# Down products of two experts as three 16-bit products instead of one in float32

## The reference

```
h    = layernorm(attention @ Wo)
gate = softmax(h @ gate_w + gate_b)                      # 8 experts
hid  = gelu(einsum('bsd,edf->bsef', h, w1) + b1)         # up product, f = 512
out  = einsum('bsef,efd->bsed', hid, w2) + b2            # down product
moe  = einsum('bse,bsed->bsd', gate, out)
```

## Time and profile before

| | |
|---|---|
| Median of 3 runs | 1122.25 us (1120.18 to 1125.5) |
| Profiled execution, its own time | 1120.17 us |
| Its span, first to last instruction | 1118.4 us |
| Granted TensorE clock over the span | 0.986 |
| Busy: PE, PEld, DVE | 96%, 82%, 86% |
| Busy: ACT, POOL | 70%, 25% |

### The profile page before, as it was taken

One profiled execution on the slowest core, in us unless ns is written; L12 is line 12 of the kernel. 1 busy time (PEld: TensorE's weight loads), 2 busy tenths in 40 slices (PEclk: granted clock), 3 DMA queues, 4 the chain that ended last, 5 costly groups with the idle time before them and its releaser, 6 DMA issues.

```text
span 1118.4 us, 27576 instructions
## 1 busy us (share of the span) xinstructions
PE 1075.0 (96%) x10435; PEld 912.2 (82%) x10435; DVE 959.6 (86%) x2543; ACT 778.9 (70%) x1772; POOL 277.7 (25%) x328
## 2 busy tenths in 40 slices
PE   4877999999999999999999999999999999999997
PEld 1664888888888888888888888888888888888897
DVE  8988798898988989898898989889898888988763
ACT  5873948668595876859677594867759587685653
POOL 2340314224031231404123140412403132140200
PEclk9995999999999999999999999999999999999999
DMA  7010000000000000000000000000000000000000
GB/s 210 7 39 10 2 11 7 1 16 1 11 7 11 6 2 16 1 11 6 6 11 2 11 7 11 6 1 16 2 11 6 11 7 6 6 6 1 7 2 10
DMA packets 18722, 14.60 MB, mean 13 GB/s; under 512 B 2408, under 2 KB 16160, under 8 KB 18592
## 3 DMA queue, kind: packets, MB, share of 16 engines
q1 hardware_dynamic: 17680, 12.76, 3.8%
q10 hardware_dynamic: 912, 0.09, 0.1%
HBM read 10.75 MB, written 2.10 MB: 11 GB/s over the span
## 4 chain that ended last, share of the span: by engine, by line
PE 89%; DVE 4%; issue 3%; ACT 2%; POOL 1%; SPq 0%; DMA 0%; POOLq 0%; DVEq 0%; ACTq 0%
PE O L565 19%; PE O L468 14%; PE S L484 5%; PE U L547 5%; PE U L548 5%; PE U L549 5%; PE J L382 5%; PE S L449 4%; PE J L343 4%; PE U L449 4%; PE S L404 4%; PE J L344 3%; PE J L345 3%; PE S L400 3%; PE O L475 2%
## 5 line engine op out<-in xcount | busy, mean ns | idle before, releaser
L777 ACT ACTIVATE hid<-U,b1c 128x256 f32<-128x256 f32 x512 | 200.5, 474 | 174.8 <-PE U L549 174.7
L565 PE MATMUL O<-w2s,hid 128*128 128x128 f32 x2048 | 251.1, 276 | 0.0
L565 PEld LDWEIGHTS O<-w2s,hid 128*128 128x128 f32 x2048 | 238.6, 192 | 2.9
L928 POOL TENSOR_SCALAR_AFFINE_SELECT P<-P 128x512 f32<-128x512 f32 x128 | 85.0, 664 | 618.6 <-ACT P L750 618.5
L468 PEld LDWEIGHTS O<-Vx,P 128*128 128x128 f32 x1536 | 188.0, 192 | 30.2 <-issue 14.3
L468 PE MATMUL O<-Vx,P 128*128 128x66 f32 x1536 | 188.6, 273 | 3.6 <-POOL P L928 2.0
L1198 DVE TENSOR_TENSOR_SCAN st<-aexp,u 128x256 f32<-128x256 f32 x256 | 178.8, 698 | 0.4 <-issue 0.3
L920 POOL TENSOR_TENSOR raw<-raw,nr 128x512 f32<-128x512 f32 x124 | 132.8, 1097 | 134.9 <-DVE nr L1066 134.9
L1208 DVE SCALAR_TENSOR_TENSOR y<-st,bc,y 128x256 f32<-128x256 f32 x240 | 133.5, 556 | 8.5
L547 PE MATMUL U<-h2h,w1h 128*128 128x256 f16 x480 | 130.9, 273 | 0.0
L549 PE MATMUL U<-h2h,w1l 128*128 128x256 f16 x480 | 130.9, 273 | 0.0
(11 more groups left out here) (204 smaller groups left out, 2048.0 us busy)
## 6 DMA issues: line engine op xcount, KB each, us to landing
xin<-in_L_attn_x SPq DMA_DIRECT2D x16, 128.0 KB, 2.1
xres<-in_L_attn_x SPq DMA_DIRECT2D x16, 128.0 KB, 2.3
hid<-in_L_ffn_w SPq DMA_DIRECT2D x2, 1024.0 KB, 6.5
out_dram<-fin SPq DMA_DIRECT2D x16, 128.0 KB, 1.8
raw<-in_L_ffn_Wq SPq DMA_DIRECT2D x1, 512.0 KB, 4.7
raw<-in_L_ffn_Wk SPq DMA_DIRECT2D x1, 512.0 KB, 6.4
raw<-in_L_ffn_Wv SPq DMA_DIRECT2D x1, 512.0 KB, 7.4
wos<-in_L_ffn_Wo SPq DMA_DIRECT2D x1, 512.0 KB, 11.4
```

What stands on the lines that cost most here:

```text
L565: last = mm(O[e % 2][:, t * P:(t + 1) * P], hid[:, e % 2, m, t * P:(t + 1) * P], w2s[:, e * FC + m, :], start=(m == 0), stop=(m == FC - 1))
L777: fn(hid[:, e % 2, f % FC, :], U[q % 2][:, m * SEQ:(m + 1) * SEQ], ACT.Gelu_apprx_tanh, bias=b1c[:, f:f + 1], scale=1.0 / WS).then_inc(gel ...
```

## The change

For experts 0 and 1 (`NH = 2`) the down product is made from 16-bit halves, as the up product is. ACT copies the gelus' values of one expert, 128x1024, to 16 bits (`hidh`), DVE subtracts that from `hid` into `hidl`, and PE makes three 16-bit matmuls where one float32 matmul was. There is one buffer each of `hidh` and `hidl`, so the copy for expert 1 waits for expert 0's down block. The halves of `w2` are made once, and scaled by 64, which the gate's copy `gate64` takes out. Line numbers of the changed kernel differ.

```diff
+        hidh = sb("hidh", [P, FC, SEQ], F16)
+        hidl = sb("hidl", [P, FC, SEQ], F16)
+        w2h = sb("w2h", [P, NH * FC, D], F16)
+        w2l = sb("w2l", [P, NH * FC, D], F16)
+        gate64 = sb("gate64", [P, T, NH])
...
             def expert_down(s, e, weighed):
-                pe.wait_ge(gelu_done, s * NE * FC + FC * (e + 1))
+                if e < NH:
+                    pe.wait_ge(hid_low, s * NH + e + 1)
+                    pe.wait_ge(w2_low, 1)
+                else:
+                    pe.wait_ge(gelu_done, s * NE * FC + FC * (e + 1))
...
                 for t in range(T):
                     for m in range(FC):
-                        last = mm(O[e % 2][:, t * P:(t + 1) * P], hid[:, e % 2, m, t * P:(t + 1) * P],
-                                  w2s[:, e * FC + m, :], start=(m == 0), stop=(m == FC - 1))
+                        dst, f, q = O[e % 2][:, t * P:(t + 1) * P], e * FC + m, slice(t * P, (t + 1) * P)
+                        if e < NH:
+                            mm(dst, hidh[:, m, q], w2h[:, f, :], start=(m == 0), stop=False)
+                            mm(dst, hidh[:, m, q], w2l[:, f, :], start=False, stop=False)
+                            last = mm(dst, hidl[:, m, q], w2h[:, f, :], start=False, stop=(m == FC - 1))
+                        else:
+                            last = mm(dst, hid[:, e % 2, m, q], w2s[:, f, :], start=(m == 0), stop=(m == FC - 1))
...
+            def hidden_high(s, e):
+                act.wait_ge(gelu_done, s * NE * FC + FC * (e + 1))
+                from_one(act, w2_ready, s * NE + e if e > 0 else (s - 1) * NE + NH)
+                fn(hidh[:, :, :], hid[:, e % 2, :, :], ACT.Copy).then_inc(hid_high, 1)
...
+                    if not old and m == 5:
+                        act.wait_ge(d_w2, 16)
+                        fn(w2h[:, :, :], w2s[:, 0:NH * FC, :], ACT.Copy, scale=WS).then_inc(w2_high, 1)
...
+                    for t in range(T):
+                        V.tensor_scalar(gate64[:, t, :], ge[:, t, 0:NH], grs[:, t:t + 1], 1.0 / WS, ALU.mult,
+                                        ALU.mult).then_inc(o_vec, 1)
...
+            def hidden_low(s, e):
+                dve.wait_ge(hid_high, s * NH + e + 1)
+                V.tensor_tensor(hidl[:, :, :], hid[:, e % 2, :, :], hidh[:, :, :], ALU.subtract).then_inc(hid_low, 1)
+
+            def split_w2():
+                dve.wait_ge(w2_high, 1)
+                V.scalar_tensor_tensor(w2l[:, :, :], w2s[:, 0:NH * FC, :], WS, w2h[:, :, :], ALU.mult, ALU.subtract
+                                       ).then_inc(w2_low, 1)
...
+                    if i == 1 and k == 7:
+                        split_w2()
```

More of the change, by code:

```diff
@@ L24 @@
 NL = NP
+NH = 2
 VW = DH + 2
@@ L35 @@
 KN = 8
-KO, KOA = 17, 2
+KO, KOA = 19, 2
 KE = 9
@@ L186, in build @@
             wo_ready wo_copied o_vec o_root o_act o_tr o_gate o_gT o_b2
-            w1_ready gelu_done w2_ready acc_done
+            w1_ready gelu_done hid_high hid_low w2_high w2_low w2_ready acc_done
             c_vec dt_ready tanh_done a_done scan_done y_done
@@ L197, in build @@
          wo_ready, wo_copied, o_vec, o_root, o_act, o_tr, o_gate, o_gT, o_b2,
-         w1_ready, gelu_done, w2_ready, acc_done,
+         w1_ready, gelu_done, hid_high, hid_low, w2_high, w2_low, w2_ready, acc_done,
          c_vec, dt_ready, tanh_done, a_done, scan_done, y_done,
@@ L526, in gated_b2 @@
             def gated_b2(s):
-                pe.wait_ge(o_vec, s * KO + 16)
+                pe.wait_ge(o_vec, s * KO + 18)
                 for t in range(T):
@@ L876, in body @@
                         copy_output(i)
+                    if old and m == 0:
+                        hidden_high(i - 1, 0)
+                    if not old and m == 5:
+                        act.wait_ge(d_w2, 16)
+                        fn(w2h[:, :, :], w2s[:, 0:NH * FC, :], ACT.Copy, scale=WS).then_inc(w2_high, 1)
                     if not new and m == 6:
@@ L885, in body @@
                         gelus(i - 1, m)
+                    if old and m == 1:
+                        hidden_high(i - 1, 1)
                     if new and m == 8:
@@ L894, in tail @@
                     gelus(LAST, e)
+                    if e < NH:
+                        hidden_high(LAST, e)
             bodies(prologue, body, tail)
@@ L1169, in add_expert @@
                     V.scalar_tensor_tensor(sum_of(s)[:, t, :], O[e % 2][:, t * P:(t + 1) * P],
-                                           gates_of(s)[:, t, e:e + 1], sum_of(s)[:, t, :], ALU.mult, ALU.add
+                                           (gate64 if e < NH else gates_of(s))[:, t, e:e + 1],
+                                           sum_of(s)[:, t, :], ALU.mult, ALU.add
                                            ).then_inc(acc_done, 1)
+            def hidden_low(s, e):
[5 more added lines that the diff above has]
+                                       ).then_inc(w2_low, 1)
             def convolve(s, n):
@@ L1364, in body @@
                         o_step(i - 1, 15)
+                        hidden_low(i - 1, 1)
                     if old and m >= 2:
@@ L1383, in body @@
                         o_step(i - 1, 14)
+                        hidden_low(i - 1, 0)
                     if new and m > 0 and m in TURN_AT:
@@ L1422, in tail @@
                         e_step(LAST - 1, n)
+                    if e < NH:
+                        hidden_low(LAST, e)
                     add_expert(LAST, e)
```

## The result

| | before | after |
|---|---|---|
| Median, same chip, 4 runs each | 1121.28 us (1120.18 to 1125.5) | 1141.32 us (1136.85 to 1143.32) |
| Ratio of the means, 95% interval | | 1.0166 (1.0125 to 1.0207) |
| Span of the profiled execution | 1118.4 us | 1139.2 us |
| Two middle sequences apart | 66.20 us | 67.14 us |

The changed kernel is slower by 20 us by the medians (18.6 by the means, which the ratio goes by). The forecast of 1136 us had the direction and its range held the time; the forecast of +14.8 us was too small. The last line of the table is the distance between the starts of two neighbouring sequences' y turns, the transposes that bring the scan's y back (569.83 and 636.03 us before, 580.02 and 647.17 us after).

The account below looks back on a forecast made before the run. PE was taken to bound the kernel, with DVE, its feeder, nearly full. 14 middle sequences gave +11.9 us and the end +2.9, in all +14.8 on 1120.17, 1135.0; between bases 1135 and 1137 the forecast was 1136, range 1127 to 1147.

Parts of the forecast that it names:

- What PE gains: Down block on PE: 24 16-bit matmuls at 0.0575 us, 1.38 us instead of 1.79, saving 0.41 per block.
- Rival b: 16-bit block no faster, loads hidden only in part: 1139 to 1141 us; with no overlap 1.7 per sequence, 1150; 15%.
- the third wait of 0.2: PE's wait at the score product of 611.76 for DVE's second maxima, 0.2 us per middle sequence.
- Steps 1 and 2, the hold: First expert's copy on ACT, then DVE's subtraction, held until one POOL product ends; DVE's next work 1.72 us late.
- Rival a: No hold by POOL on the first subtraction: 0.5 us per sequence, +9.9, 1130 to 1132 us; 12%.
- c: POOL holds the first subtraction over its whole run of four products: 2.5 us per sequence, +38, 1158 us; 4%.
- Steps 3 to 5, the waits: PE waits 0.5 for first maxima, 0.8 for second subtraction, 0.2 and 0.1 for later maxima; 0.85 us later per sequence.
- the fourth wait, of 0.1: PE's wait at the score product of 620.03 for DVE's maxima, 0.1 us per middle sequence.
- Step 4: Second expert's subtraction queues on DVE behind the accumulator copy, y giving back 0.29; second block waits 0.8 us.
- step 5: DVE's first accumulator addition 2.41 us late; gaps absorb part, later maxima make PE wait 0.2 and 0.1.
- The end: Last body and tail: blocks wait for copy and subtraction, less 0.82 saved each: +1.1 and +1.8 us.
- Rivals d and e: d: subtraction in about 0.6 us, 1107 to 1116, 8%; e: DVE's gaps larger in other sequences, 1119 to 1127, 8%.

Follow-up runs that it names:

- Run 4: The changed kernel with GpSimd's four products of the next sequence held back until the first subtraction is done: 1155.41 us, ratio 1.0282 to the kernel before.
- Run 2: The changed kernel with all copies and subtractions still made, but float32 down blocks that wait for the gelus alone: 1139.05 us, ratio 1.0121 to the kernel before.
- run 6: The changed kernel with 16-bit down products for expert 1 alone: 1117.33 us, ratio 0.9937 to the kernel before.
- run 7: The changed kernel with 16-bit down products for expert 0 alone: 1125.01 us, ratio 1.0 to the kernel before.
- run 8: The changed kernel with all eight experts in 16 bits, without low halves of the gelus' values, 16 matmuls a block: 1076.85 us, ratio 0.9572 to the kernel before.
- run 10: The changed kernel with the last two sequences' down products all in float32: 1138.58 us, ratio 1.0127 to the kernel before.
- runs 1: The changed kernel without DVE's two subtractions per sequence, low halves set to zero once: 1108.14 us, ratio 0.9852 to the kernel before.

## Why the prediction was right in direction and too small in size

- **What PE gains:** right. A block is 1.35 us by the earlier trace rows's price 1.38; 24 matmuls in a row run at 0.056 us each. The 81 ns per matmul of 128 columns that the Trainium skill gives ("TensorE: Matmul & The Clock Gate", section "Back-to-back issue gap") don't hold here, where 0.056 us was measured. Rival b falls by the 1.35 us. (By the walk's own steps its case without overlap is 1.5 us per sequence, not 1.7, as the third wait of 0.2 would go; no chance hangs on it.)
- **Steps 1 and 2, the hold:** right. The first subtraction began 0.01 from where I put it (613.55 less 10.19 is 603.36) and the next work 0.06 from it (the step's own numbers, 603.8 and 1.14, give 604.94 and not the 604.85 that it went on with). Run 4 shows the hold by taking POOL away: 1.22 instead of 1.50. Rival a falls; so does c, as the subtraction was held for part of one product and not for the run of four. The rule that I had drawn on, by which a DVE instruction with two SBUF inputs and a GpSimd one that reads SBUF get in each other's way (the Trainium skill, "SBUF — State Buffer", section "Who interferes with whom"), agrees with run 4. That the hold lasts for a whole instruction is said there of another mode of DVE; here POOL's third product agrees with it, 2.02 us instead of 1.04.
- **Steps 3 to 5, the waits:** the places, the order and the releasers came as forecast, 0.60, 0.73 and 0.27 us of idle time, and 26.6 us new in all, where I asked for over 20; the fourth wait, of 0.1, did not come. Step 4 was 0.11 short: y gave back its 0.29, but the scan ahead of it met POOL's next operation (616.91, 0.72 us long) and took 0.90 instead of 0.68. The total of +0.85 per middle sequence measured +0.94.
- **How I put the cause:** too narrow. I booked each wait of PE as a cost and the blocks as a gain against it. Run 2 shows that block speed and waits are one account: without the fast blocks nothing is lost, because DVE's list alone sets the pace. "0.82 saved, 1.6 waited" gave nearly the right sum because step 5 carried DVE's delay through to the last score product; in run 2, with nothing saved and one listed wait of 0.74 us, the sequences are the same 67.14 us apart.
- **Mis-sized: the weights' split, "0 to 1.2, I take 0".** Between the first two y turns the changed kernel is 1.81 us longer than the kernel before with the like start (68.17 and 66.36), 0.87 beyond the middle's 0.94. The timeline of all engines there in the changed kernel, with VectorE's row of the split, GpSimd's mask and TensorE's wait for that:

```profile
129.24 2.06 DVE L1213 SCALAR_TENSOR_TENSOR w2l<-w2s,w2h 128x1024 f16<-128x1024 f32 x1
...
130.17 1.62 POOL L958 TENSOR_SCALAR_AFFINE_SELECT P<-P 128x512 f32<-128x512 f32 x1
...
131.84 1.55 PE L474 MATMUL O<-Vx,P 128*128 128x66 f32 x12 [0.61 <-POOL P L958]
```

  and GpSimd's mask in the ninth run, the kernel before:

```profile
130.25 0.64 POOL L928 TENSOR_SCALAR_AFFINE_SELECT P<-P 128x512 f32<-128x512 f32 x1
```

  The split lay in a DVE gap of 1.08 us of before, but beside POOL, whose mask took 0.98 us longer, and PE waits for that. I had looked for cover on DVE's own queue only. No run leaves the split out, but three change its length. With one expert's weights (run 6; run 7 the same) and with all eight (run 8) the mask at this place is

```profile
131.41 1.09 POOL L958 TENSOR_SCALAR_AFFINE_SELECT P<-P 128x512 f32<-128x512 f32 x1
```

```profile
130.24 4.82 POOL L939 TENSOR_SCALAR_AFFINE_SELECT P<-P 128x512 f32<-128x512 f32 x1
```

  PE's list of waits for the mask has no new one in runs 6 and 7, one of 0.61 in the changed kernel and one of 3.8 us in run 8. So the cause of the 0.61 is shown; the remaining 0.26 of the 0.87 stays open.
- **The end:** right in the sum. +2.9 was forecast for the waits there, run 10 measures 2.96: 0.9 in the last body and 2.0 in the tail, where 1.1 and 1.8 were forecast.
- **Not in the sum: the clock.** 1.55 us in the last body, and on the first chip a start that was slow in the changed kernel's profile and not in before's. No edit is shown to cause either.
- **The account of the 18.0 us** between like profiles: 13 middle intervals of 0.94 are 12.2, less 0.57 since two of before's are 0.28 longer than the rest; the first interval 1.81; the last 4.51 (2.96 and 1.55); together 17.95. The medians say 20.0 (first chip) and 17.1 (second). The 3 us between the two could be the start: before's median is 1121.3 on the first chip and 1125.3 on the second, after's 1141.3 and 1142.3. That isn't shown: before has one profile on the first chip, none on the second, and one on another.
- Rivals d and e: refuted by 1.21 us for an undisturbed subtraction, nearly twice the 0.65 from which d decides, and by 67.14 in every middle interval.

## What to carry to other kernels

Before work is moved from a busy engine to its feeder, add up the feeder's gaps between two of its deadlines in the stretch where the work will stand: here none between the gate copy and the first maxima and 1.7 us behind, for 2.7 us of subtractions, so expert 1's split, which stands behind those maxima, fits (0.6% faster), expert 0's, ahead of them, eats its gain, and both together lose 1.5%. What PE saves beyond the feeder's pace is worth nothing, and a test that keeps the feeder's new work and undoes the saving shows that at once. Look at who shares SBUF with the new operation as well as at its own queue, and compare profiles with like starts before a difference of a few microseconds is explained.

## What the runs showed of the hardware beyond that

- DVE operations on two SBUF tensors and POOL's operations prolong each other, and not only DVE's `TENSOR_TENSOR`: the scan went from 0.68 to 1.44 us, y from 0.48 to 1.08, POOL's four products from 4.04 to 5.03, its mask from 0.64 to 1.62, and to 4.82 beside a DVE operation of 5.26 us. The order of the lists decides who pays, as in run 4.
- The granted clock fell to its lower level within some 3 us of the same place of the last body in the five profiles with sequences 67.14 us apart, and in none of the others there (both of before and runs 1, 4, 6, 7, 8). PE's rows in the 15 us ahead of it are alike in the changed kernel and in before. In the changed kernel's profile that is 1.55 us, which no edit at that place explains.
